# Attention score matmuls: from 128-row operands with zero rows to 32 rows a head, on one Trainium2 core

## The chip, the cores and the metric

The program runs on one core of a Trainium2 chip. Its engines work side by side, each through its own list of instructions in order: TensorE (PE; PEld is its weight load), VectorE (DVE), ScalarE (ACT), GpSimd (POOL) and SyncE (SP), which issues most of the DMAs. They wait for each other through semaphores. The metric is the device time of one execution in microseconds (us); less is better.

## The reference, cut to what matters

One block: gated cross-attention of 16 heads with 8 channels each, over 32 sequences of 128 tokens with 128 channels, and then a gated mixture of experts. The change is in the first part.

```python
B, S, D = 32, 128, 128; H = 16; HD = D // H          # of the inputs used
q = proj(layernorm(x), Wq, bq); k = proj(ctx, Wk, bk); v = proj(ctx, Wv, bv)
scores = jnp.einsum('bhqd,bhkd->bhqk', q, k) / math.sqrt(HD)
scores = jnp.where(m == 0, jnp.float32(-10000000000.0), scores)
p_attn = jax.nn.softmax(scores, axis=-1)
o = jnp.einsum('bhqk,bhkd->bhqd', p_attn, v)         # back to 128 channels
x = x + jnp.tanh(g_xattn[0]) * (o @ Wo + bo)
# then: layernorm, 2 shared and 8 routed experts (two a token), x + tanh(g_ffn[0]) * (...)
```

## The kernel before, in words

**Stages.** A prologue loads x and ctx and finds scales; the attention follows; then the shared experts and the routed experts run with PE nearly always busy. The weights of the experts are loaded and split into two f16 parts during the attention.

**Turns and steps.** The attention works on 16 pairs of sequences. `turns` calls each engine's `body(t, ...)` for turns t = 0 to 19, and each body goes through 8 steps g = 0 to 7 (G = 8). A pair passes through several turns: its q and k are projected at the end of turn t - 1, its plain scores are made from step 2 of turn t + 1 on, its shifted scores from step 7 of turn t + 2 on. A group is 4 heads of one sequence, so a pair has 8 groups and a step handles one plain group and one shifted group. The order on each engine is as the code is written; nothing moves it at run time except the waits.

**What a pair needs.**
- PE transposes x and ctx (L853, L855), ACT copies them out (`XCT`, L645), PE projects q and k (L860, L861, `project_queries_keys`), ACT scales them into `QK32` (L653, `queries_keys`).
- POOL splits them into a high and a low f16 part (L529, L531), then normalises the next pair (L521), adds a bias row (L596), splits weights for the experts (L541, L543, L545, from turn 6 on) and from turn 8 on prepares the rows of the experts (`payload`, L555 to L560), always in this order.
- SP writes the parts to DRAM (`scr`, L453, L455), adds the key mask (L432), and reads them back in another layout: `Q` with 64 rows for two heads (L473) and `K` as two DMAs (L476), each into the half of the rows that belongs to even or odd heads; the other half of `K` stays zero from the start. An f16 row holds high or low parts of one channel, so 32 rows of a head give a product of nearly f32 accuracy. A DMA from Q to Q (L465) clears the rows for the row maxima.
- PE makes the **plain scores** of a group in 4 matmuls (`plain`, L880, into `pS`, two buffers), DVE takes their row maxima (L1257). When the pair's 8 groups are done, PE transposes the maxima (L933), ACT and DVE split them (L676, L1263), and SP puts them into Q as extra rows (L470). The **shifted scores**, transposed (`less`, L880, into `pE`, two buffers), then come out with the row's maximum taken off.
- ACT takes the exponentials (L735, into `PT`, 4 buffers), and PE multiplies them with the values (`values`, L919), two groups every second step, as four 32-column matmuls side by side. The rest of the pair is transposed (L939, L945), projected with Wo (L949) and added to x by DVE (L1276).

**Waits.** A score matmul of group n waits for the maximum or exponential of group n - 2. DVE also computes the inverse deviations for the experts, four linked rounds of small operations in turns 8, 12, 16, 18 and 20 (L1291 to L1302); POOL's payload waits for them.

Of the kernel before, what the change touches and what calls it, by code (L numbers as in the profile page):

```python
# [13 lines left out]
P = 128  # L14
# [20 lines left out]
SLOT_ROWS = 4 * HD  # L35
SHIFT = 2 * SLOT_ROWS
# [10 lines left out]
MASK16 = BIG16 / HD  # L47
# [54 lines left out]
def prologue(nc, io, k):  # L102

    with ExitStack() as ctx:
# [19 lines left out]
        with nc.Block() as block:  # L124
# [11 lines left out]
            def _(g):  # L136
# [6 lines left out]
                g.memset(k.constk[:], BIG16)  # L143
                clear_keys(g, k, 0).then_inc(s.init, 1)
                g.wait_ge(s.init, 1)
                for m in (k.identf, k.ident16):
# [5 lines left out]
                                pattern=[[1, P]], channel_multiplier=-1)  # L152
                for u in range(1, NB - 1):
                    ins = clear_keys(g, k, u)
                ins.then_inc(s.init, 1)
# [17 lines left out]
            def _(v):  # L173
                link = Chain(v, s.dv)
                for u in range(2):
                    link(clear_pair(v, k, u))
                    ins = ones_of_values(v, k, u)
# [21 lines left out]
def clear_keys(g, k, u):  # L199
    return g.memset(k.K[u][:].rearrange("p a b -> p (a b)").bitcast(F32), 0.0)  # L200


def clear_pair(v, k, u):

    v.memset(k.V[u][:].rearrange("p a b c -> p (a b c)"), 0.0)
    return v.memset(k.Q[u][:].rearrange("p a b -> p (a b)").bitcast(F32), 0.0)
# [21 lines left out]
def layer(nc, io, k):  # L228
# [11 lines left out]
    NPT = 4  # L240
# [17 lines left out]
    in_pair = lambda t: t[0:2 * HD].rearrange("p (a b) -> p a b", a=2)  # L258
    MPT = [[in_pair(hi), bg(f"MPl{u}", [2 * HD, 2, S], F16)[:]] for u, hi in enumerate((k.constk, k.constq))]
# [40 lines left out]
    shifts = pA[1][0:2 * HD, 0:2, :]  # L300
# [15 lines left out]
    N_W, N_RD, N_M = 16 * 3, 16 * 4, 16 * 2  # L316
# [11 lines left out]
    head = lambda g, j: 4 * j + g % 4  # L328
# [64 lines left out]
    with nc.Block() as block:  # L393
        @block.sync
        def _(sp):
            head_dim, operand = 4 * W2T, P * 4 * W2T

            def load_tokens(n):
                tiles = slice(CHUNK * n, CHUNK * (n + 1))
                sp.dma_start(k.X[:, tiles, :], io.x.rearrange("b s d -> s b d")[:, tiles, :]).then_inc(k.s_x[n], 16)  # L400
# [27 lines left out]
            def key_mask(t):  # L428
# [3 lines left out]
                sp.dma_start(k.scr[u][1, :, 3, :], k.kmd[t * W2T:(t + 1) * W2T].partition_broadcast(P)).then_inc(s.w[u], 16)  # L432
# [9 lines left out]
            for u in range(NB):  # L442
                if u == NB - 1:
                    sp.wait_ge(s.zk, 1)
                for par in range(2):
                    sp.dma_start(k.K[u][SHIFT + 2 * par:SHIFT + 2 * par + 2, par::2, :], k.constk[:]).then_inc(k.s_padk, 16)

            def body(t, a, b, c, o):
# [10 lines left out]
                if a:  # L459
                    if t == 0:  # L460
                        sp.wait_ge(k.s_pad, 16 * NB)
                    if t == 2:
                        sp.wait_ge(s.z, 1)
                    wait(sp, s.ST, G * (t - NB + 1))
                    sp.dma_start(k.Q[u][SHIFT:SHIFT + 4, :, :], k.Q[u][SHIFT + 4:SHIFT + 8, :, :]).then_inc(s.rd[u], 16)  # L465
                if b:
                    v = (t - 2) % NB
                    for n, done in ((0, s.t2), (1, s.mp)):
                        sp.wait_ge(done, t - 1)
                        sp.dma_start(k.Q[v][SHIFT + n:SHIFT + 4:2, :, :], MPT[t % 2][n].rearrange("p a b -> p (a b)")).then_inc(s.m[v], 16)  # L470
                if a:
                    sp.wait_ge(s.w[u], N_W * again + N_W)
                    sp.dma_start(k.Q[u][0:SHIFT, :, :], scr[0].rearrange("(h2 pd) s t -> (pd s) h2 t", pd=2 * HD)).then_inc(s.rd[u], 16)  # L473
                    for par in range(2):
                        src = scr[1].rearrange("(h2 par d) s t -> par (d s) h2 t", par=2, d=HD)[par]
                        sp.dma_start(k.K[u][SLOT_ROWS * par:SLOT_ROWS * (par + 1), par::2, :], src).then_inc(s.rd[u], 16)  # L476
# [8 lines left out]
                for n in range(2):  # L485
                    if t == TOPS_STORED[n]:
                        store_tops(n)
                for n in {15: range(0, 3), 16: range(3, 6), 17: range(6, NE)}.get(t, ()):
# [27 lines left out]
        def _(g):  # L516
# [59 lines left out]
            def body(t, a, b, c, o):  # L576
                if t < LAG:
                    normalise(t + 1)
                if t == 0:
                    clear_keys(g, k, NB - 1)  # L580
# [1060 lines left out]
```

## Time and profile before

| what | value |
| --- | --- |
| times of 3 runs | 465.22, 465.64, 468.93 us; median 465.64 |
| profiled execution, span from first to last instruction | 464.5 us |
| busy: PE, DVE, ACT, POOL | 392.2, 387.9, 341.6, 316.3 us (84, 84, 74, 68%) |
| DMA | 53.22 MB, mean 115 GB/s |

Only the span of the profiled execution was recorded, not its own device time; the span is 0.7 us under the fastest of the three runs and 1.1 us under their median. Busy shares are means over stages with different limits, so they say little; the stage is read by its own window. In the rows below, "idle" and "waited for" name what ended the wait. Durations of matmuls contain the fill and drain of the array; successive matmuls overlap, so the rate is read from start to start.

### The profile page before, as it was taken

To read this page: it belongs to the slowest core of one execution; us is meant where nothing else is said; L and a number is where in the kernel's file an instruction comes from. 1 tells how busy PE (TensorE), PEld (TensorE's weight loads), DVE (VectorE), ACT (ScalarE), POOL (GpSimd) and SP (SyncE) were. 2 spreads that over 40 slices of the span, in tenths; PEclk is the share of its full clock that TensorE was granted. 3 is DMA by queue.
4 is the path that set the end of the run, shared out by engine and by line. 5 is a ranking of instruction groups with operands and counts; after the bars stand their busy time and mean duration, and the time that the engine had idled before them with its cause. 6 is when DMAs were issued, how large, how long until landed. Compare 5 with 4: busy or idle time off the path is not lost.

```text
span 464.5 us, 13551 instructions
## 1 busy us (share of the span) xinstructions
PE 392.2 (84%) x4611; PEld 297.0 (64%) x4611; DVE 387.9 (84%) x951; ACT 341.6 (74%) x674; POOL 316.3 (68%) x439
## 2 busy tenths in 40 slices
PE   0457998997999899987789897999999999999910
PEld 0335777785887787765534343444699999999910
DVE  7596678978777977799696799777799999999986
ACT  0635687787888788877668657888688888888854
POOL 6242222799899999978777777775067777777750
PEclk9999999999999999999899899999999999999975
DMA  7978884354444253555001111111313333355229
GB/s 190 285 209 222 187 182 107 89 135 95 107 101 105 61 119 92 148 213 185 26 6 53 51 53 46 46 51 55 80 60 93 101 90 97 90 147 171 73 67 295
DMA packets 71825, 53.22 MB, mean 115 GB/s; under 512 B 7481, under 2 KB 63620, under 8 KB 71760
## 3 DMA queue, kind: packets, MB, share of 16 engines
q1 hardware_dynamic: 64752, 43.02, 34.9%
q0 software_dynamic: 4544, 8.44, 5.5%
q10 hardware_dynamic: 2464, 0.91, 0.8%
q8 instruction: 39, 0.64, 0.6%
q14 instruction: 26, 0.21, 0.2%
HBM read 29.38 MB, written 24.33 MB: 116 GB/s over the span
## 4 chain that ended last, share of the span: by engine, by line
PE 46%; DVE 22%; POOL 12%; issue 5%; DMA 5%; ACT 4%; SPq 2%; DVEq 0%; POOLq 0%; ACTq 0%
PE pAtt L1143 11%; PE pAtt L1080 6%; PE pS L1131 5%; PE pE L1131 5%; PE pS L1018 3%; DVE HH L1508 3%; PE pE L1018 3%; DVE t_MX L1257 3%; DMA scr<-QKS 2%; PE pS L880 2%; PE pMix L1121 2%; POOL t_STG L541 2%; POOL t_W2l L545 2%; POOL QKS L531 2%; PE pAtt L919 1%
## 5 line engine op out<-in xcount | busy, mean ns | idle before, releaser
L637 POOL DMA_INDIRECT yd<-Y,XR x78 | 86.8, 1113 | 40.6 <-issue 23.2
L1257 DVE TENSOR_REDUCE t_MX<-pS 128x4 f32<-128x512 f32 x128 | 86.9, 682 | 22.7 <-PE pS L880 20.2
L735 ACT ACTIVATE PT<-pE,t_mbias,t_scl 128x512 f32<-128x512 f32 x128 | 97.0, 789 | 2.9 <-PE pE L880 2.7
L611 POOL DMA_INDIRECT xs<-t_STG,t_pos x64 | 65.6, 1024 | 21.5 <-issue 14.8
L1536 DVE SCALAR_TENSOR_TENSOR HR<-G,t_sc,HR 128x512 f16<-128x512 f32 x78 | 58.6, 751 | 2.8
L1143 PE MATMUL pAtt<-t_W2h,HR 128*128 x624 | 59.2, 219 | 0.8 <-DVE HR L1536 0.7
L880 PE MATMUL pS<-t_K,t_Q 128*128 128x128 f16 x512 | 52.5, 229 | 7.8 <-DVE t_MX L1257 5.1
L1508 DVE SCALAR_TENSOR_TENSOR HH<-H,t_sc,HH 128x512 f16<-128x512 f32 x64 | 48.2, 764 | 8.2 <-ACT HH L789 6.3
L1143 PE MATMUL pAtt<-t_W2l,HR 128*128 x312 | 54.4, 219 | 0.0
L820 ACT ACTIVATE G<-pS,t_b1T,t_inv 128x256 f32<-128x256 f32 x78 | 40.0, 563 | 17.1 <-PE pS L1131 16.1
L880 PE MATMUL pE<-t_Q,t_K 128*128 128x128 f16 x512 | 50.2, 221 | 1.9 <-DMA t_Q<-MPl 1.0
L1143 PEld LDWEIGHTS pAtt<-t_W2h,HR 128*128 128x128 f16 x624 | 49.6, 98 | 1.4 <-issue 1.4
L1080 PE MATMUL pAtt<-HH,t_W2h 128*128 128x512 f16 x128 | 38.4, 381 | 6.8 <-DVE HH L1508 6.8
L880 PEld LDWEIGHTS pS<-t_K,t_Q 128*128 128x128 f16 x512 | 35.6, 103 | 12.6 <-DVE t_MX L1257 7.7
L919 PE MATMUL pAtt<-PT,t_V 128*32 128x128 f32 x1024 | 42.0, 283 | 0.0
L880 PEld LDWEIGHTS pE<-t_Q,t_K 128*128 128x128 f16 x512 | 37.4, 99 | 6.6 <-ACT PT L735 3.4
L820 ACT ACTIVATE G<-pE,t_b1T,t_inv 128x256 f32<-128x256 f32 x78 | 39.9, 569 | 0.0
L1534 DVE TENSOR_SCALAR HR<-G,t_sc 128x512 f16<-128x512 f32 x78 | 37.9, 485 | 0.8 <-ACT G L820 0.2
L529 POOL CAST QKS<-QK 128x512 f16<-128x512 f32 x16 | 9.8, 611 | 42.0 <-ACT QK L653 42.0
L784 ACT ACTIVATE H<-pS,t_b1T,t_inv 128x512 f32<-128x512 f32 x32 | 23.7, 777 | 12.0 <-PE pS L1018 8.0
L1131 PE MATMUL pE<-XE,t_W1h 128*128 128x256 f16 x156 | 32.1, 273 | 0.0
L1131 PE MATMUL pS<-XE,t_W1h 128*128 128x256 f16 x156 | 31.9, 273 | 0.0
(276 smaller groups left out, 1008.6 us busy)
## 6 DMA issues: line engine op xcount, KB each, us to landing
xs<-t_padrow SPq DMA_DIRECT2D x10, 516.0 KB, 5.0
XR<-xs SPq DMA_DIRECT2D x39, 129.0 KB, 2.3
scr<-QKS SPq DMA_DIRECT2D x16, 256.0 KB, 2.4
t_Q<-scr SPq DMA_DIRECT2D x16, 256.0 KB
t_K<-scr SPq DMA_DIRECT2D x32, 128.0 KB
t_STG<-in_W SPq DMA_DIRECT2D x7, 512.0 KB, 6.8
YY<-yd SPq DMA_DIRECT2D x14, 256.0 KB, 4.9
t_X<-in_x SPq DMA_DIRECT2D x4, 512.0 KB, 6.1
```

Of the source, the lines that this page charges most:

```text
L611: g.indirect_dma_start(k.xs, bass.IndirectOffsetOnAxis(ap=pos[:, n:n + 1], axis=0), k.PAY[:, n, :], None).then_inc(h.di[q], 16)
L637: g.indirect_dma_start(k.yd, bass.IndirectOffsetOnAxis(ap=XR[u][:, q, D:ROW], axis=0), Y[u][:, q, :], None, bounds_check=2 * T - 1, oob_is ...
L735: act.activation(PT[:, m % NPT], pE[g % 2][:], ACT.Exp, bias=k.mbias[:, bt:bt + 1], scale=k.scl[:, bt:bt + 1]).then_inc(s.exp, 1)
L820: act.activation(G32[i % 2][:, c, :], pU[c][:, 0:TILE], ACT.Gelu, bias=k.b1T[:, bass.ds(e * NC + c, 1)], scale=k.inv[:, 3:4]).then_inc(r.g ...
L880: ins = pe.matmul(out[:, j, :], ko if transposed else qo, qo if transposed else ko, start=True, stop=True)
L919: ins = pe.matmul(pA[bb][32 * j:32 * j + 32, part // 2, :], k.V[pair % NB][:, 4 * bb + j, part, :], PT[:, m % NPT, j, :], start=(part == 0 ...
L1080: ins = pe.matmul(wide(pA[u]), w[:, w0:w0 + P], HH[e][:, part, c, :], start=(e == 0 and c == 0 and step == 0), stop=(e == 1 and c == NC - ...
L1131: ins = pe.matmul(pU[c][:, 0:TILE], w[:, bass.ds(e * HID + c * P, P)], XE[i % M][:, part, :], start=(step == 0), stop=(step == 2))
L1143: ins = pe.matmul(pA[i % 2][:, q, :], HR[i % M][:, part, c, q * P:(q + 1) * P], w[:, bass.ds(e * HID + c * P, P)], start=(c == 0 and q == ...
L1257: v.tensor_reduce(out=MX[:, n // G % 2, n % G // 4, m % 2, m // 2::2], in_=pS[n % 2][:], axis=AX_X, op=ALU.max).then_inc(s.max, 1)
L1508: v.scalar_tensor_tensor(out=HH[e][:, 1, c, :], in0=H32[:, c, :], scalar=k.sc[:, 2:3], in1=HH[e][:, 0, c, :], op0=ALU.mult, op1=ALU.subtra ...
L1536: v.scalar_tensor_tensor(out=HR[i % M][:, 1, ch, :], in0=G32[i % 2][:, ch, :], scalar=k.sc[:, 2:3], in1=HR[i % M][:, 0, ch, :], op0=ALU.mu ...
```

## The change: what it does

Q and K get one layout: 4 groups of 32 rows, one head in each, 4 heads side by side along the free dimension (`[128, 4, 256]`). A score matmul uses the 32 rows of its head alone, on one of four row groups of the array, and there are no zero rows; the memsets that made them are gone from POOL, DVE and ACT. K comes in one DMA instead of two, and the clearing DMA from Q to Q is gone, since the zeros come with the constants from DRAM: 12 DMAs of 32 KB at the start instead of 4 of 64 KB and 8 small ones. The constants of the mask stand in 4 rows a head instead of 8, so the mask's DMA halves.

`scores(n, m)` replaces `plain` and `less`: it waits for both buffers first and then issues the 4 shifted and 4 plain matmuls in turn, which always lie in different row groups, and signals after the last of each. `values` run four groups at a time at steps 0 and 4 (8 buffers `PT` instead of 4). The projection of q and k, its copy on ACT, the second output projection and the second `residual` move one step later.

```diff
-SLOT_ROWS = 4 * HD
-SHIFT = 2 * SLOT_ROWS
+ROWS = 4
+HEAD_ROWS = P // ROWS
+MASKED = 4
+SHIFT = 4 * HD - 5
...
-    NPT = 4
+    NPT = 8
...
-    N_W, N_RD, N_M = 16 * 3, 16 * 4, 16 * 2
+    N_W, N_RD, N_M = 16 * 3, 16 * 2, 16 * 2
+    SETS = 3
...
+            def fourth(u, op):
+                return k.scr[u][op, :, 3, :].rearrange("(h d) t -> h d t", d=HD)
...
             for u in range(NB):
-                sp.dma_start(k.scr[u][0, :, 3, :], k.constq[:]).then_inc(k.s_pad, 16)
+                sp.dma_start(fourth(u, 0)[:, 0:MASKED, :], k.constq[:]).then_inc(k.s_pad, 16)
+                sp.dma_start(fourth(u, 0)[:, MASKED:HD, :], k.nothing[:]).then_inc(k.s_pad, 16)
+                sp.dma_start(fourth(u, 1)[:, MASKED:HD, :], k.constk[:]).then_inc(k.s_pad, 16)
...
-                    sp.dma_start(k.Q[u][SHIFT:SHIFT + 4, :, :], k.Q[u][SHIFT + 4:SHIFT + 8, :, :]).then_inc(s.rd[u], 16)
...
-                        sp.dma_start(k.Q[v][SHIFT + n:SHIFT + 4:2, :, :], MPT[t % 2][n].rearrange("p a b -> p (a b)")).then_inc(s.m[v], 16)
+                        row = SHIFT + 4 * n
+                        sp.dma_start(k.Q[v][row:row + P - HEAD_ROWS + 1:HEAD_ROWS, :, :], MPT[t % 2][n].rearrange("p a b -> p (a b)")).then_inc(s.m[v], 16)
...
-                    sp.dma_start(k.Q[u][0:SHIFT, :, :], scr[0].rearrange("(h2 pd) s t -> (pd s) h2 t", pd=2 * HD)).then_inc(s.rd[u], 16)
-                    for par in range(2):
-                        src = scr[1].rearrange("(h2 par d) s t -> par (d s) h2 t", par=2, d=HD)[par]
-                        sp.dma_start(k.K[u][SLOT_ROWS * par:SLOT_ROWS * (par + 1), par::2, :], src).then_inc(s.rd[u], 16)
+                    for op, into in ((0, k.Q[u]), (1, k.K[u])):
+                        sp.dma_start(into[:], scr[op].rearrange("(j rd) s t -> (rd s) j t", rd=ROWS * HD)).then_inc(s.rd[u], 16)
...
-                    if g == 6 and 2 <= t < NP - 1:
+                    if g == 7 and 2 <= t < NP - 1:
                         queries_keys(t + 1)
...
+            def score(n, j, out, transposed):
+                g, u = n % G, n // G % NB
+                rows, q = slice(HEAD_ROWS * (g % ROWS), HEAD_ROWS * (g % ROWS + 1)), S * (g // 4)
+                qo, ko = k.Q[u][rows, j, q:q + S], k.K[u][rows, j, q:q + S]
+                return pe.matmul(out[:, j, :], ko if transposed else qo, qo if transposed else ko, start=True, stop=True)
+
+            def scores(n, m):
+                plain, less = 0 <= n < G * NP, 0 <= m < G * NP
+                if less:
+                    if m % G == 0:
+                        pe.wait_ge(s.m[m // G % NB], N_M * (m // G // NB) + N_M)
+                    wait(pe, s.exp, m - 1)
+                if plain:
+                    if n % G == 0:
+                        pe.wait_ge(s.rd[n // G % NB], N_RD * (n // G // NB) + N_RD)
+                    wait(pe, s.max, n - 1)
                 for j in range(4):
...
+                    if less:
+                        to = score(m, j, pE[m % 2], True)
+                    if plain:
+                        of = score(n, j, pS[n % 2], False)
+                if less:
+                    to.then_inc(s.ST, 1)
+                if plain:
+                    of.then_inc(s.S, 1)
...
-                    less(m + 1)
-                    plain(G * (t - 1) + g - PH + 1)
-                    if g % 2 == 0:
-                        values(m - 2)
-                        values(m - 1)
+                    scores(G * (t - 1) + g - PH + 1, m + 1)
+                    if g % 4 == 0:
+                        for n in range(m - 4, m):
+                            values(n)
...
-                    if g == 5 and 2 <= t < NP - 1:
+                    if g == 6 and 2 <= t < NP - 1:
                         project_queries_keys(t + 1)
-                    if g == 5 and o:
+                    if g == 6 and o:
                         project_output(1, t - LAG - 1)
...
-                    if g == 6 and o:
+                    if g == 7 and o:
                         residual(1, pair - 1)
```

How the instructions stand. On **PE**, steps 4 to 6 of an early turn; pE takes shifted and pS plain scores. Before:

```order
L919 MATMUL pAtt<-PT,t_V 32x128 x8
L945 MATMUL pOut<-t_identf,t_AK 128x128
L853 MATMUL pMix<-t_identf,XN 128x128 x2
L855 MATMUL pMix<-t_identf,t_W2l 128x128 x2
L880 MATMUL pE<-t_Q,t_K 128x128 x4
L880 MATMUL pS<-t_K,t_Q 128x128 x4
L860 MATMUL pMix<-XCT,t_Wq 128x256
L861 MATMUL pMix<-XCT,t_Wk 128x256
L949 MATMUL pOut<-t_Wo,t_AT 128x128
```

and with the change:

```order
L907 MATMUL pAtt<-PT,t_V 32x128 x16
L933 MATMUL pOut<-t_identf,t_AK 128x128
L842 MATMUL pMix<-t_identf,XN 128x128 x2
L844 MATMUL pMix<-t_identf,t_W2l 128x128 x2
L870 MATMUL pE<-t_Q,t_K 128x128
L870 MATMUL pS<-t_K,t_Q 128x128
...
L849 MATMUL pMix<-XCT,t_Wq 128x256
L850 MATMUL pMix<-XCT,t_Wk 128x256
L937 MATMUL pOut<-t_Wo,t_AT 128x128
```

The two score rows stand eight times there, that is for steps 5 and 6: a whole step of scores now lies between the transposes and the projections, which lay behind the scores of step 5.

On **SP**, the DMAs of one early turn. Before:

```order
L453 DMA scr<-QKS 128x2x512
L455 DMA scr<-QKS 128x2x256
L432 DMA scr<-kmd 128x256
L465 DMA t_Q<-t_Q 4x2048
L470 DMA t_Q<-t_constk 2x8x256
L470 DMA t_Q<-MPl 2x8x256
L473 DMA t_Q<-scr 64x8x256
L476 DMA t_K<-scr 32x8x256 x2
```

and with the change:

```order
L447 DMA scr<-QKS 128x2x512
L449 DMA scr<-QKS 128x2x256
L429 DMA scr<-kmd 16x4x256
L462 DMA t_Q<-t_constk 4x4x256
L462 DMA t_Q<-MPl 4x4x256
L466 DMA t_Q<-scr 128x4x256
L466 DMA t_K<-scr 128x4x256
```

Two of nine DMAs a turn are gone, and the mask's is half as large.

## Rows read from the trace of the kernel before

**Rows 1.** Busy us by engine in six stretches; the first line names the columns.

```profile
core 0: us, PE busy (x) PEld busy (x) DVE busy (x) ACT busy (x) POOL busy (x), PEclk, DMA share, GB/s
52.30:83.10 30.80, 27.95 (x421) 22.62 (x418) 24.64 (x60) 24.30 (x51) 9.69 (x15) 1.00 0.73 168
83.10:115.80 32.70, 28.64 (x439) 23.23 (x428) 28.57 (x76) 24.93 (x52) 30.32 (x55) 1.00 0.43 102
115.80:201.20 85.40, 81.25 (x1277) 66.63 (x1275) 67.65 (x180) 71.78 (x153) 77.09 (x137) 1.00 0.44 110
201.20:226.30 25.10, 20.02 (x331) 15.20 (x331) 23.34 (x84) 18.88 (x38) 19.14 (x38) 0.93 0.41 151
219.50:222.90 3.40, 0.98 (x11) 0.90 (x11) 3.08 (x13) 0.70 (x3) 2.76 (x7) 1.00 0.07 19
222.90:226.40 3.50, 3.32 (x46) 2.22 (x44) 3.13 (x15) 3.11 (x7) 1.68 (x5) 0.51 0.00 0
```

**Rows 2.** POOL's waits, 84 to 202 us: total us, times, longest.

```profile
POOL t_XF L555 <- DVE t_nmr L1302: 1.8, 2, 1.5
...
POOL QKS L529 <- ACT QK L653: 0.3, 1, 0.3
```

**Rows 3.** POOL in order of time, one turn: start, us, line and instruction.

```profile
128.29 0.89 POOL L555 TENSOR_SCALAR t_XF<-t_X,t_rstd,t_nmr 128x128 f32<-128x128 f32 x2 [0.18 <-POOL t_W2l L545]
...
130.32 0.61 POOL L529 CAST QKS<-QK 128x512 f16<-128x512 f32 x1
...
139.27 0.88 POOL L555 TENSOR_SCALAR t_XF<-t_X,t_rstd,t_nmr 128x128 f32<-128x128 f32 x2 [0.18 <-POOL t_W2l L545]
```

**Rows 4.** ACT in order of time, the copy that L529 waits for.

```profile
127.63 1.04 ACT L653 ACTIVATE QK<-pMix,t_bqk,t_sc 128x256 f32<-128x256 f32 x2
```

**Rows 5.** The chain that ended last, 52 to 84 us: start, us, what.

```profile
54.27 3.95 DMA scr<-QKS
...
59.58 0.45 SPq L476
...
61.27 2.81 SPq L416
...
64.61 5.46 DMA scr<-QKS
...
71.44 4.63 DMA t_K<-scr
...
81.64 0.68 DVE t_MX L1257
```

**Rows 6.** SP in order of time, 53 to 73 us: the clearing DMA.

```profile
65.72 0.67 SPq L465 DMA_DIRECT2D t_Q<-t_Q  x1
```

**Rows 7.** PE in order of time, step 0 of one turn.

```profile
129.39 0.40 PE L880 MATMUL pE<-t_Q,t_K 128*128 128x128 f16 x4
129.63 0.39 PE L880 MATMUL pS<-t_K,t_Q 128*128 128x128 f16 x4
129.94 0.65 PE L919 MATMUL pAtt<-PT,t_V 128*32 128x128 f32 x16
130.52 0.40 PE L958 MATMUL pMix<-t_ident,t_STG 128*128 128x128 f16 x4
```

**Rows 8.** PE's waits, 83.2 to 202 us, for the load of K.

```profile
PE pS L880 <- DMA t_K<-scr: 1.0, 1, 1.0
```

**Rows 9.** The chain that ended last, 14 to 39 us.

```profile
15.28 4.61 DVE t_mx L196 x4
...
37.20 0.85 PE pMix L861 x2
38.05 0.44 PE pS L880 x4
```

**Rows 10.** SP in order of time, 20 to 29 us: constants at the start.

```profile
20.48 2.39 SPq L439 DMA_DIRECT2D scr<-t_constq  x4
...
23.58 5.40 SPq L446 DMA_DIRECT2D t_K<-t_constk  x8
```

More of the change, by code:

```diff
@@ L46 @@
 BIG16 = 32768.0
-MASK16 = BIG16 / HD
+MASK16 = BIG16 / MASKED
 class Parts(dict):
@@ L151, in _ @@
                 g.affine_select(out=k.lower[:], in_=k.lower[:], compare_op=ALU.is_gt, fill=0.0, base=0,
[L152 to L155, printed above, removed]
+                                pattern=[[1, P]], channel_multiplier=-1).then_inc(s.init, 1)
                 g.wait_ge(s.init, 2)
@@ L874, in _ @@
             pe.matmul(bias_cols, bvr[:], k.Wo[:], start=True, stop=True).then_inc(s.any, 1)
-            def scores(g, u, out, transposed):
-                for j in range(4):
-                    hd, q = head(g, j), S * (g // 4)
-                    qo, ko = k.Q[u][:, hd // 2, q:q + S], k.K[u][:, hd, q:q + S]
-                    ins = pe.matmul(out[:, j, :], ko if transposed else qo, qo if transposed else ko, start=True, stop=True)
-                return ins
-            def plain(n):
-                if not 0 <= n < G * NP:
-                    return
-                pair, g = n // G, n % G
-                if n == 0:
-                    pe.wait_ge(k.s_padk, 32 * NB)
-                if g == 0:
-                    pe.wait_ge(s.rd[pair % NB], N_RD * (pair // NB) + N_RD)
-                wait(pe, s.max, n - 1)
-                scores(g, pair % NB, pS[n % 2], False).then_inc(s.S, 1)
@@ L895, in less @@
-            def less(m):
-                if not 0 <= m < G * NP:
-                    return
-                pair, g = m // G, m % G
-                if g == 0:
-                    pe.wait_ge(s.m[pair % NB], N_M * (pair // NB) + N_M)
-                wait(pe, s.exp, m - 1)
-                scores(g, pair % NB, pE[m % 2], True).then_inc(s.ST, 1)
+            def score(n, j, out, transposed):
[3 more added lines that the diff above has]
+                return pe.matmul(out[:, j, :], ko if transposed else qo, qo if transposed else ko, start=True, stop=True)
@@ L1599, in program @@
         k.s_c, k.s_x = ([outer.enter_context(nc.semaphore(f"{n}{c}")) for c in range(NT // CHUNK)] for n in ("c_ctx", "c_x"))
-        k.s_one, k.s_pad, k.s_padk, k.s_b2, k.s_rest = (outer.enter_context(nc.semaphore("c_" + n)) for n in ("one", "pad", "padk", "b2", "rest"))
+        k.s_one, k.s_pad, k.s_b2, k.s_rest = (outer.enter_context(nc.semaphore("c_" + n)) for n in ("one", "pad", "b2", "rest"))
         k.keep = outer
-        alloc(outer, k, MX=([P, 2, 2, 2, HD], F32), PV=([P, 2, 2, S], F32),
+        alloc(outer, k, MX=([P, 2, 2, ROWS, 4], F32), PV=([P, 2, 2, S], F32),
               REC=([P, 2, H], F32), AK=([P, 2, H, HD], F32), AT=([P, 2, S], F32), ST6=([P, 2, 6], F32), XF=([P, 2, D], F32),
```

44 lines of the change are left out of this document (16 added, 28 removed).

## The prediction, made before the changed kernel was run

> **What bounds the kernel now.** I cut the attention into stretches and read the busy times in each first [rows 1]. PE looks like the bound of all of them: 27.95 of 30.8 us, 28.64 of 32.7, 81.25 of 85.4. But POOL is as full between 83.1 and 201.2 us: 30.32 of 32.7 and 77.09 of 85.4. To tell which of two full engines leads, I read who waits for whom. From 84 to 202 us POOL waits 1.8 us for DVE's inverse deviations and 0.3 us for the copy of q and k, and for nothing else but itself [rows 2]. An engine that stands still for 2 us in 118 runs at its own pace. Its order of time shows that pace: the same instruction stands at 128.29 and at 139.27 us, a turn of 10.98 us [rows 3]. Its little gaps are linked operations waiting for each other, and the change does not touch POOL's list there. PE's work is 81.25 / (85.4 / 10.98) = 10.45 us a turn, 0.5 us less than POOL's: PE follows.
>
> Before 83.1 us POOL has little to do (9.69 of 30.8 us), so something else leads there. The chain that ended last runs from 54 to 76 us through SP and DMAs: the write of the parts 3.95 us, issues of K, of weights and of the maxima (2.81 us), the next write 5.46 us, the load of K 4.63 us [rows 5]. PE, 91% busy in that stretch, appears in it only at the end. After 201.2 us DVE leads: 23.34 of 25.1 us [rows 1]. So the change speeds up the engine that is fullest, and that leads in none of the three stretches.
>
> **The change part by part.**
>
> *Scores on 32 rows.* A group's four matmuls start 129.63 - 129.39 = 0.24 us before the next four, so a step's eight take 0.48 us and a turn's 64 take 3.84 us [rows 7]; their weight loads are already hidden, since that is 0.06 us each. The trace has no matmul on a row group, so the price is bounded: if the two row groups do not overlap, nothing is saved; if they overlap fully, half, 1.92 us a turn. The nearest row is the values: 16 matmuls on four column groups start and are over in 0.58 us, four side by side [rows 7]. I take nearly the full 1.9 us. The Trainium skill, "TensorE: Matmul & The Clock Gate", Part 3, says the same of row groups: matmuls on different ones run at once, four tiles measured 3.07 times faster. No run here shows it yet.
>
> *Values four groups at a time.* A block of two takes 0.58 us, and 0.07 us are lost before it (0.31 from the plain scores to the values against 0.24 between two sets of scores) [rows 7]. Half as many blocks save four such losses, 0.3 us a turn. A block of four makes PE deaf to scores for 1.2 us; ACT and DVE have up to two finished groups in their buffers, about 1.4 us of work.
>
> *Changes between tile shapes.* Before, only the values differ in shape: four blocks, eight changes a turn. Now scores (32 rows), values (32 columns) and all other matmuls (full) differ from each other: counted in the new order, three changes at steps 0 and 4, two at 1, 2, 3 and 6, 14 a turn. At 0.07 us, six more cost 0.4 us; at a whole matmul's 0.24 us [rows 7], 14 x 0.24 - 8 x 0.07 = 2.8 us. I take 0.4 us, the row of a change of shape. In sum PE has 1.9 + 0.3 - 0.7 (the four value losses are in both counts, so I keep a margin) = 1.5 us a turn less to do, about 9 us a turn.
>
> *What this is worth from 83.1 to 201.2 us:* nothing by itself, POOL's 10.98 us stand. At most the 1.8 us that POOL waits for DVE can go, because DVE gets its maxima sooner: 0 to 1.8, I take 1.3 us. DVE has the room, 28.57 of 32.7 us.
>
> *Projections one step later.* A step is 10.98 / 8 = 1.4 us. POOL needs the copy of q and k at 130.32 us and has it at 127.63 + 1.04 = 128.67 us [rows 3, 4]: 1.65 us to spare, more than a step, and PE gains on it. Cost there nothing. Late next, if that cover were gone, is POOL's L529, with the split weights behind it: the excess over 1.65 us would be paid in each of some nine turns.
>
> *SP.* K's second issue is gone: 0.45 us in the chain in turn 3, and again before the load of K in turn 4, 0.9 us in all [rows 5]. The clearing DMA's 0.67 us issue [rows 6] lies beside the 5.46 us write that SP waits for anyway: nothing. The bytes of a turn are nearly the same. Against the 0.9 us stands the later projection in turn 5: now behind the scores of step 6, which wait for the maximum that DVE ends at 81.64 + 0.68 us [rows 5]. That may cost up to a step, 1.4 us, less what the faster scores give back. For the stretch before 83.1 us: from a loss of 1.4 us to a gain of 3 turns x 1.9 = 5.7 us if PE led after all. I take a gain of 0.3 us, near the SP rows, since the chain names SP.
>
> *Prologue.* The memsets of K, Q and constants lie beside the loads of ctx; the chain from 15 to 38 us is DVE's maxima, PE and ACT [rows 9]. Nothing. The constants' DMAs: 4 took 2.39 us and 8 took 5.40 us to issue, 7.8 us; 12 at 0.60 to 0.68 us take 7.2 to 8.1 [rows 10]. They end before the first scores, which stand directly behind the projection of pair 2 on PE [rows 9]. Nothing.
>
> *The last pair.* Once in 118 us PE waited for the load of K, 1.0 us [rows 8]; with one issue less I take 0.5 us (0 to 1.0).
>
> *The end, 201.2 to 226.3 us:* DVE's idle time is 25.1 - 23.34 = 1.76 us, the most that faster scores can give. I take 0.7 us. What follows starts that much earlier and is not changed.
>
> **Sum.** 0.3 + 1.3 + 0.5 + 0.7 = 2.8 us. The span was 464.5 us, 1.1 us under the median of the runs, 465.64; taken off that, 462.8 us. By the bounds: 465.64 + 1.4 = 467.0 at one end, 465.64 - 5.7 - 1.8 - 1.0 - 1.8 = 455.3 at the other.
>
> **The rivals.**
>
> *PE led before 83.1 us.* For it: 91% busy, more than any other engine there. Against: the chain. Then 3 x 1.5 to 1.9 us come off early and all of POOL's work moves forward; with 1.8 + 0.5 to 1.0 + 0.7 to 1.8 us behind: 7.5 to 10.3 us less, 455.3 to 458, say 456.8. Chance 0.20.
>
> *No overlap of row groups.* Then PE saves only 0.3 us a turn, and shape changes take that back. POOL still leads; what stays is SP's part, 0.5 to 1 us: 465. For it: no row shows a row group at work. Chance 0.17.
>
> *Slower: shape changes make PE the leader.* For it: 14 changes against 8, and scores stand between nearly all other matmuls. It decides from the point where PE's turn passes 10.98 us, 0.5 us more than now. At 0.24 us a change and no overlap, PE's turn is 10.45 + 2.8 = 13.2 us, 2.3 us over POOL's in 7.8 turns, and as much in the three early ones: some 20 us; at half that price and no overlap, 10.45 + 1.1 = 11.6 us, 0.6 us in some ten turns, 6 us. So 472 to 485, say 474. Against: the 0.07 us row. The Trainium skill, "TensorEngine Tiling (Array Packing)", section "Tiling Modes", has this rule: a change of tiling mode, not just of the tile, drains TensorE. The values' 0.07 us shows a loss of that kind, though a small one. Chance 0.11.
>
> *The clock falls.* PE was 0.98 of 3.4 us busy from 219.5 us, and the next 3.4 us had a granted clock of 0.51 of 2.4 GHz, that is 1.2 GHz [rows 1]. If a PE with less to do fell so once a turn, 3.4 us at half speed take 1.7 us of its work; PE's 9 us become 10.7, still under 10.98. So it matters only if it stays low, and then PE's turn is near 18 us and the time over 550. Against: at 9 us a turn PE would still be over 80% busy, and a stretch at 28.64 of 32.7 us held 1.00. Chance 0.03.
>
> **The numbers.** The forecast, POOL leads and PE's gain turns into waiting: 0.49, with its own range 459.5 to 465. The likeliest time is 462.8 us. About 1%, 4.7 us, is what a measurement here can tell from no change, so faster begins at 461.0. Of the forecast a quarter lies there (0.13), with the 0.20 of the first rival: 0.33. Slower is the third rival and the fourth, 0.14. The rest, 0.53, is the same. A range from 456.0 to 468.5 leaves out the slow cases and part of the early gain, together 0.2.
>
> **What the profile would show.** Right, if POOL's turn stays at 10.98 us with no new wait for L653, PE's busy share between 83 and 201 us falls from 95% toward 85%, and PE's new idle time is put down to POOL's L521 or to the load of K. Scores: eight starts within 0.25 to 0.3 us, pE and pS nearly together; if they still take 0.48 us, the rows do not overlap. Shape changes: the start-to-start time from scores to the next full matmul and back; over 0.2 us speaks for the slower rival. DVE's wait at L555 should go from 1.8 us toward 0. I am wrong if POOL's list starts its turn 6 over 2 us before 83.1 us, if POOL waits for L653 in the middle turns, or if the granted clock drops below 1.00 before 219 us.

## The result and the profile after

The changed kernel took 475.91 us (median of 4 runs, 471.89 to 478.14); the kernel before 465.88 us beside it. The ratio is 1.022, with a 95% interval of 1.015 to 1.029: 2.2% slower, outside the range that was given (456.0 to 468.5 us). Four further runs, taken later, gave 476.44 us, 1.027 (1.020 to 1.034). Medians here are of all runs; ratios and their intervals leave out runs more than 1.5% above the fastest of the same kernel. Engines and clock of the profiled execution (span 476.3 us, 478.14 us by its own time), from the page; each digit is a fortieth of the span:

```profile
PE 396.5 (83%) x4611; PEld 285.0 (60%) x4611; DVE 383.0 (80%) x949; ACT 339.8 (71%) x672; POOL 307.9 (65%) x436
...
PEclk9999999896899689855589999999999999999975
```

The granted clock of the kernel before, for comparison:

```profile
PEclk9999999999999999999899899999999999999975
```

PE's busy time rose by 4 us although its scores take half as long. The second line goes with that: the granted clock has dips that the kernel before does not have. The same in stretches of the clock's record, busy us by engine:

```profile
core 0: us, PE busy (x) PEld busy (x) DVE busy (x) ACT busy (x) POOL busy (x), PEclk, DMA share, GB/s
...
83.90:87.30 3.40, 3.40 (x52) 2.39 (x50) 3.37 (x10) 1.80 (x3) 2.23 (x4) 0.50 0.00 0
107.80:111.20 3.40, 2.52 (x33) 1.39 (x32) 3.19 (x10) 2.87 (x9) 3.33 (x6) 1.00 0.41 126
111.20:121.50 10.30, 8.09 (x82) 5.99 (x83) 7.99 (x26) 4.96 (x10) 7.83 (x16) 0.50 0.20 58
121.50:159.00 37.50, 31.91 (x574) 23.33 (x568) 28.02 (x73) 32.89 (x72) 34.62 (x62) 1.00 0.31 90
155.60:159.00 3.40, 2.26 (x36) 1.33 (x32) 3.19 (x10) 3.06 (x10) 3.25 (x7) 1.00 0.39 120
159.00:169.30 10.30, 9.00 (x93) 6.67 (x97) 7.08 (x21) 5.36 (x10) 6.78 (x13) 0.50 0.19 56
...
200.00:240.90 40.90, 39.85 (x449) 28.03 (x440) 28.93 (x104) 25.66 (x51) 27.96 (x52) 0.50 0.38 134
```

Four stretches, 65 us together, stand at 0.50, that is 1.2 GHz. Ahead of the second and third PE had little to do: 2.52 and 2.26 of 3.4 us, while DVE had 3.19 in both, in turns 8 and 12 with their rounds of inverse deviations. But little work alone does not bring a fall. Here are a stretch of the kernel before, in turn 8 too, and another of the changed kernel; the clock fell behind neither:

```profile
107.80:111.20 3.40, 2.36 (x39) 1.88 (x38) 3.19 (x10) 2.60 (x7) 3.19 (x7) 1.00 0.95 207
```

```profile
128.20:131.60 3.40, 2.37 (x28) 1.82 (x26) 1.50 (x4) 3.23 (x7) 3.02 (x7) 1.00 0.54 158
```

In the last of the four PE is busy for 39.85 of 40.9 us: at half speed it leads the tail, in which DVE led before [rows 1].

The clock was also late. Its record begins at 52.3 us before and at 60.0 us after; the windows print 1.00 ahead of that, which is no measurement. Matmuls in order of time tell it:

```profile
55.32 0.31 PE L870 MATMUL pE<-t_Q,t_K 32*128 32x128 f16 x1
55.35 0.31 PE L870 MATMUL pS<-t_K,t_Q 32*128 32x128 f16 x1
55.42 0.31 PE L870 MATMUL pE<-t_Q,t_K 32*128 32x128 f16 x1
...
134.10 0.27 PE L933 MATMUL pOut<-t_identf,t_AK 128*128 128x128 f32 x1
134.30 0.23 PE L870 MATMUL pE<-t_Q,t_K 32*128 32x128 f16 x1
134.31 0.22 PE L870 MATMUL pS<-t_K,t_Q 32*128 32x128 f16 x1
134.37 0.21 PE L870 MATMUL pE<-t_Q,t_K 32*128 32x128 f16 x1
...
134.48 0.21 PE L870 MATMUL pS<-t_K,t_Q 32*128 32x128 f16 x1
134.63 0.44 PE L927 MATMUL pAtt<-t_identf,t_PV 128*128 128x128 f32 x2
```

At 55 us two pE scores start 0.10 us apart, at 134 us 0.06 to 0.07: half clock, then full. The rows show two more things. pE and pS start together, so the row groups overlap: eight scores take 0.24 us, not 0.48. And a change of shape has a price: the first score starts 0.20 us after a transpose, the next transpose 0.15 us after the last score. In the kernel before, where both have 128 rows, it was 0.11:

```profile
131.25 0.27 PE L945 MATMUL pOut<-t_identf,t_AK 128*128 128x128 f32 x1
131.36 0.39 PE L880 MATMUL pE<-t_Q,t_K 128*128 128x128 f16 x4
```

That is 0.09 us for the way there, where 0.07 was taken; the way back costs as much, 0.15 against the 0.06 between two scores.

POOL's casts of q and k after, as in [rows 3]:

```profile
132.55 0.61 POOL L521 CAST QKS<-QK 128x512 f16<-128x512 f32 x1
...
143.49 0.60 POOL L521 CAST QKS<-QK 128x512 f16<-128x512 f32 x1
...
154.42 0.61 POOL L521 CAST QKS<-QK 128x512 f16<-128x512 f32 x1
168.31 0.61 POOL L521 CAST QKS<-QK 128x512 f16<-128x512 f32 x1 [2.76 <-ACT QK L644]
```

At full clock POOL's turn is 10.94 us, with no wait. The turn that holds the fall at 159 us takes 13.9 us (11.1 before), and POOL waits 2.76 us for the copy.

To find where the time went, I took the same marks from the traces: the start of POOL's cast of a pair, the end of the last exponential, the end of the span. They begin at pair 2, since executions differ by 1 to 1.5 us ahead of it. The runs named keep, keep from 5 and steps back are experiments below.

| us between marks | before | after | after, again | keep | keep from 5 | keep, steps back, less tail |
| --- | --- | --- | --- | --- | --- | --- |
| cast of pair 2 to 6 | 43.9 | 45.9 | 45.9 | 46.0 | 46.3 | 45.4 |
| 6 to 12 | 69.5 | 69.4 | 69.0 | 69.1 | 69.9 | 73.4 |
| 12 to 13 | 11.1 | 13.9 | 12.6 | 12.3 | 12.2 | 12.5 |
| 13 to 15 | 22.0 | 22.5 | 21.9 | 21.9 | 21.9 | 21.9 |
| 15 to last exponential | 39.7 | 47.4 | 46.5 | 43.0 | 40.0 | 41.5 |
| to the end | 239.2 | 238.1 | 238.0 | 237.5 | 239.4 | 239.2 |
| low clock from 60 to 241 us | 3.4 | 64.9 | 47.8 | 3.4 | 0 | 13.7 |

The spans differ by 11.7 us (476.25 against 464.53). Of these 7.7 are lost in the tail, 2.8 in the turn of pair 12, 2.0 in the first turns and 0.5 behind pair 13; 1.1 come back at the end.

The tail can be followed through four executions without any added matmuls in it. With 13.7 us of low clock between the cast of pair 15 and the last exponential it took 41.9 us (warm start, an experiment below), with 23.9 us 44.2 (apart, below), with 34.7 us 46.5 (after, again) and with 38.1 us 47.4 (after). In the kernel before it was 39.7 us with 2.4.

### The profile page after: what moved, and what is told of

Its sections match the earlier page's. It is cut to its first block, busy times and chain, and to the rows that moved or that the text cites. A ratio compares the mean times of both kernels' runs of the same rounds, so it can differ in the third digit from the quotient of the medians.

```text
span 476.3 us, 13605 instructions
## 1 busy us (share of the span) xinstructions
PE 396.5 (83%) x4611; PEld 285.0 (60%) x4611; DVE 383.0 (80%) x949; ACT 339.8 (71%) x672; POOL 307.9 (65%) x436
## 4 chain that ended last, share of the span: by engine, by line
PE 61%; DVE 16%; ACT 8%; issue 7%; DMA 2%; POOL 1%; SPq 0%; ACTq 0%; POOLq 0%; DVEq 0%
PE pAtt L1130 9%; PE pAtt L907 8%; PE pE L870 6%; PE pAtt L1067 5%; PE pS L1118 5%; PE pE L1118 5%; ACT PT L724 4%; DVE HH L1495 3%; PE pS L1006 3%; PE pE L1006 3%; PE pMix L849 3%; DVE t_MX L1244 3%; PE pMix L850 2%; PE pMix L1108 2%; PE pOut L937 1%
## 5 line engine op out<-in xcount | busy, mean ns | idle before, releaser
L870 PE MATMUL pE<-t_Q,t_K 32*128 32x128 f16 x512 | 55.4, 242 | 22.7 <-ACT PT L724 17.4
L870 PEld LDWEIGHTS pE<-t_Q,t_K 32*128 32x128 f16 x512 | 33.6, 103 | 45.9 <-ACT PT L724 29.9
L1495 DVE SCALAR_TENSOR_TENSOR HH<-H,t_sc,HH 128x512 f16<-128x512 f32 x64 | 48.2, 764 | 7.8 <-ACT HH L778 5.9
L870 PE MATMUL pS<-t_K,t_Q 32*128 32x128 f16 x512 | 51.3, 243 | 1.9 <-DVE t_MX L1244 1.9
L907 PE MATMUL pAtt<-PT,t_V 128*32 128x128 f32 x1024 | 43.7, 324 | 0.0
L809 ACT ACTIVATE G<-pE,t_b1T,t_inv 128x256 f32<-128x256 f32 x78 | 39.7, 567 | 0.0
L907 PEld LDWEIGHTS pAtt<-PT,t_V 128*32 128x32 f32 x1024 | 32.1, 129 | 5.1 <-issue 2.0
L870 PEld LDWEIGHTS pS<-t_K,t_Q 32*128 32x128 f16 x512 | 30.2, 102 | 5.1 <-DVE t_MX L1244 3.8
```

The costliest lines, as they stand in the source:

```text
L809: act.activation(G32[i % 2][:, c, :], pU[c][:, 0:TILE], ACT.Gelu, bias=k.b1T[:, bass.ds(e * NC + c, 1)], scale=k.inv[:, 3:4]).then_inc(r.g ...
L870: return pe.matmul(out[:, j, :], ko if transposed else qo, qo if transposed else ko, start=True, stop=True)
L907: ins = pe.matmul(pA[bb][32 * j:32 * j + 32, part // 2, :], k.V[pair % NB][:, 4 * bb + j, part, :], PT[:, m % NPT, j, :], start=(part == 0 ...
L1495: v.scalar_tensor_tensor(out=HH[e][:, 1, c, :], in0=H32[:, c, :], scalar=k.sc[:, 2:3], in1=HH[e][:, 0, c, :], op0=ALU.mult, op1=ALU.subtra ...
```

## The experiments

**First four: undo one part each, or give PE its time back.** Theories: C, the granted clock; W, new waits (one wait for both scores, blocks of four); P, the later projection.

*Twice*: every score matmul issued twice.

```diff
-                for j in range(4):
+                for j in (0, 1, 2, 3) * 2:
                     if less:
                         to = score(m, j, pE[m % 2], True)
```

> The changed kernel, but every score matmul is issued a second time into the same place: PE gets the time back that the row groups saved (eight starts 0.24 us, sixteen 0.48 us) and nothing else moves. Theory C (the granted clock: a PE with less to do falls to 1.2 GHz in places, for 64 us between 84 and 241 us in the profile after, and is warm only from 60 instead of 52 us): the low stretches before 241 us shrink to under 25 us in all and the time is 460 to 467 us. Theory W (the new waits: scores wait for both buffers, values block PE for four groups): more work in the same waits, 476 us or more. Theory P (the later projection makes POOL wait 13.2 us for the copy of q and k): unchanged waits, 474 to 480 us.

488.02 us, 1.047 (1.037 to 1.056). The time is in theory W's range and against theory C as it was put: the low clock between 84 and 241 us did shrink, to 13.6 us, and the time rose. PE had its full clock at 63.9 us only, and then led: POOL's cast waits for the copy in every turn, which takes 11.67 us:

```profile
140.77 0.61 POOL L521 CAST QKS<-QK 128x512 f16<-128x512 f32 x1 [0.68 <-ACT QK L644]
152.44 0.61 POOL L521 CAST QKS<-QK 128x512 f16<-128x512 f32 x1 [0.67 <-ACT QK L644]
```

*Steps back*: the four calls at their old steps.

```diff
-                    if g == 6 and 2 <= t < NP - 1:
+                    if g == 5 and 2 <= t < NP - 1:
                         project_queries_keys(t + 1)
...
```

> The changed kernel with the projection of q and k, its copy, the second output projection and the second residual at their old steps. Theory P: POOL's 13.2 us of waits for the copy of q and k fall below 4 us, 464 to 467 us. Theory C: PE has as little to do as before, the clock falls as often, 470 to 478 us. Theory W: nothing of the waits for ACT and DVE goes, 473 to 478 us.

471.38 us, 1.014 (1.007 to 1.020); of its five runs four took 469.4 to 472.8 us and one 482.45. Between the theories. The four had a mean clock of 0.950 to 0.965, those of the changed kernel 0.914 to 0.942, so this does not separate P from C. Keep, steps back, below, does so for turn 12.

*Blocks of two*: values as before, two groups every second step.

```diff
-                    if g % 4 == 0:
-                        for n in range(m - 4, m):
+                    if g % 2 == 0:
+                        for n in range(m - 2, m):
                             values(n)
```

> The changed kernel with the values two groups at a time at every second step. Theory W: steps are even again, ACT's exponentials and DVE's maxima do not stop while a block of 1.0 us runs, 464 to 468 us. Theory C: PE's work is the same within 0.3 us a turn, low clock for as long as in the changed kernel (over 50 us before 241 us), 470 to 478 us. Theory P: 474 to 478 us.

481.13 us, 1.034 (1.027 to 1.040): slower than the changed kernel and outside all three ranges. The blocks of four are no loss.

*Apart*: shifted scores first, then plain ones, each behind its own wait.

```diff
-                    scores(G * (t - 1) + g - PH + 1, m + 1)
+                    scores(-1, m + 1)
+                    scores(G * (t - 1) + g - PH + 1, -1)
```

> The changed kernel with the shifted scores of a step issued first, behind their own wait, and the plain scores then behind theirs, as in the kernel before; rows and layout as changed. If the row groups overlap only between neighbours of different groups, eight starts take 0.45 us again instead of 0.24, PE is busier, and theory C expects less low clock than in the changed kernel and 464 to 471 us; if they overlap anyway, theory C expects 470 to 478 us. Theory W (one wait for both): 464 to 468 us whatever the clock does. Theory P: 474 to 478 us.

477.03 us, 1.028 (1.021 to 1.035): theory W falls, as far as one wait for both scores goes. The trace shows why the order within a step is free. Issued four and four, pE and pS still start side by side:

```profile
133.07 0.22 PE L870 MATMUL pE<-t_Q,t_K 32*128 32x128 f16 x1
133.09 0.23 PE L870 MATMUL pS<-t_K,t_Q 32*128 32x128 f16 x1
133.14 0.21 PE L870 MATMUL pE<-t_Q,t_K 32*128 32x128 f16 x1
133.15 0.21 PE L870 MATMUL pS<-t_K,t_Q 32*128 32x128 f16 x1
```

**The next four: the layout alone, and matmuls on all rows.** *Rows only* joins the last three edits, so that only the layout is left. *Rows only, twice* adds the doubling. *Whole first* puts matmuls on all 128 rows into the changed kernel, in steps with plain scores alone too, *rows only, whole* into the layout alone. Theory O says that the moves together cost, theory R that matmuls on 32 rows leave the clock low:

```diff
+                for j in range(4):
+                    if less:
+                        whole(m, j, pE[m % 2], True)    # score() with all 128 rows
                 for j in range(4):
                     if less:
                         to = score(m, j, pE[m % 2], True)
```

> The changed kernel with the whole order of the kernel before: projections at their old steps, values two groups at a time, shifted scores ahead of plain ones with waits of their own. Only the layout with 32 rows a head (and its DMAs and buffers) is left of the change. Theory O (the three moves together cost, each alone is covered by the others): 462 to 468 us. Theory C (PE has less to do, the granted clock falls and PE stays at 1.2 GHz longer at the start): low clock as long as in the changed kernel, first full clock after 58 us, 469 to 478 us.

> The one before with every score matmul issued twice, so that PE spends as long on scores as in the kernel before, on 32 rows. Theory O: PE's turn is as before, 464 to 469 us. Theory C as it stood (the clock follows how long PE works): clock as in the kernel before, 464 to 469 us. Theory R (it is matmuls on 32 rows that leave the clock low, as the doubling showed, where PE worked without a break and got the full clock only at 63.9 us): first full clock after 58 us, 472 to 488 us.

> The changed kernel with four matmuls on all 128 rows ahead of the eight of each step, into the place that the shifted scores then overwrite: PE's time for scores is that of the kernel before (0.24 + 0.24 us a step), as with the doubling, but half of it on all rows. Theory R: full clock from 52 to 56 us on, under 20 us of low clock between 84 and 241 us, 462 to 472 us. Theory O, and a theory that only PE's time counts: as the doubling, 480 to 492 us.

> The layout alone, in the order of the kernel before, with the four matmuls on all rows ahead of the shifted scores of each step. Theory R: clock as in the kernel before, 462 to 467 us, and clearly under the one without them. Theory O: PE has 0.24 us more a step than without, 464 to 470 us, no better than without them.

Rows only: 483.9 us, 1.042 (1.033 to 1.051), so the moves as a whole are worth 8 us under the new layout; theory O (the moves cost) falls, and theory C's 478 us is passed too. Its clock came at 79.7 us and was low for 41 us up to 243 us.

Rows only, twice: 562.0 to 600.8 us in four runs (median 589.6), far beyond any expectation. The profiled execution took 579.0 us. Its busy times by engine, and below them PE in order of time:

```profile
64.00:260.00 196.00, 196.00 (x1907) 147.38 (x1905) 83.12 (x205) 83.40 (x164) 76.92 (x137) 1.00 0.19 55
```

```profile
140.77 0.31 PE L870 MATMUL pE<-t_Q,t_K 32*128 32x128 f16 x1
140.86 0.31 PE L870 MATMUL pS<-t_K,t_Q 32*128 32x128 f16 x1
140.88 0.31 PE L870 MATMUL pE<-t_Q,t_K 32*128 32x128 f16 x1
```

PE was busy for all of 196 us and stayed at 1.2 GHz: pE starts 0.11 us apart, and the clock's record begins at 260.0 us. The printed 1.00 of that stretch, and with it this run's mean of 0.985, is a default. The Trainium skill, "TensorE: Matmul & The Clock Gate", Part 1, says that the slow clock is the default state and that activity releases it. This trace shows that being busy is not enough: with scores on 32 rows a full PE stayed slow, and in the kernel before, on 128 rows, it was fast from 52.3 us. But rows are not the whole of it. *Twice*, with the same doubled scores in the changed kernel's order, was at full clock from 63.9 us; what in the order makes this difference was not tested.

Rows only, whole: 477.8 us, 1.029 (1.022 to 1.036), 6 us faster than rows only although 32 matmuls a turn were added. Theory R's clock holds, and that the added matmuls win time, but not its 462 to 467 us. Nearly all of the 6 us lies behind the last exponential (237.6 us against 243.2, where rows only had its clock low until 243.5 and for 6.9 us more later): in the attention the held clock and the added work nearly cancel. From 67.0 to 459.5 us its clock never fell:

```profile
PEclk9999999999999999999999999999999999999985
```

At full clock it shows the price of the shapes: PE leads, a turn of POOL takes 11.64 us (casts at 149.52 and 161.16 us, the second behind a wait of 0.65 us for the copy), against 10.98 before with the same score time. It has 20 changes of shape a turn against 8; 12 more at 0.09 us are 1.1 us on PE's 10.45. Whole first: 490.1 us, 1.055 (1.047 to 1.063), in the range of the theory that only PE's time counts and not in R's, although the full clock came at 57.9 us and fell three times for 3.4 us only before 241 us: work added in every step makes PE lead. So it must be added only where PE waits.

**Four that hold the clock in places.** *Keep*: eight whole matmuls a step in turns 8, 12 and 16 to 18, between the two waits. *Warm start*: 128-row matmuls where PE waits from 16 to 52 us. *Both*, and the warm start in the kernel before. Theory C is now that the granted clock sets the loss, theory W2 that the uneven steps of the new order do. `fill` stands in several places, with 6 to 20 matmuls:

```diff
+    KEEP = {8: 8, 12: 8, 16: 8, 17: 8, 18: 8}
...
                     wait(pe, s.exp, m - 1)
+                    for j in range(KEEP.get(m // G + LAG, 0)):
+                        whole(m, j % 4, pE[m % 2], True)
                 if plain:
...
+                    fill(8)    # warm start: ident16 by ident16 into pE[0], ahead of early waits
```

> The changed kernel with eight extra matmuls on all 128 rows a step in turns 8, 12, 16, 17 and 18 (the turns in which the clock fell), between the wait for the exponential and the wait for the maximum, into the place that the shifted scores overwrite. Nothing else is changed. Theory C (the granted clock sets the loss): the early stretch stays as in the changed kernel (full clock from about 60 us), low clock between 100 and 241 us goes from 61 us to under 15, and with it the 2.7 us lost at 159 to 169 and the 7.7 us at 200 to 241: 462 to 468 us. Theory W2 (the uneven steps of the new order set PE's turn, the clock only follows): 474 us or more, since PE gets work added.

> The changed kernel with extra 128-row matmuls where PE waits between 16 and 52 us, so that it is busy on all rows before the scores begin. Theory C: full clock before 35 us, projections of the first pairs in half the time, POOL's split of pair 6 by 79 to 83 us instead of 84.9; the later falls stay: 468 to 474 us. Theory W2: the early chain through SP and DMAs and the uneven steps set the pace, pair 6 within 1 us of 84.9, 474 to 479 us.

> The changed kernel with the extra matmuls of both, and four a step in turns 3 and 4. Theory C: full clock from before 35 us to the end but for under 20 us, 456 to 464 us, faster than the kernel before. Theory W2: 472 us or more.

> The kernel before with the same extra matmuls between 16 and 52 us. Theory C: full clock before 35 us instead of 52.3, the prologue's projections in half the time, 458 to 463 us. Rival (the prologue's chain hides PE): 464 to 467 us, the same.

Keep: 470.62 us, 1.010 (1.004 to 1.016): more work on PE, and half of the loss is gone. Three of its four runs took 469.3 to 470.7 us; in the fourth, 479.26 us, the mean clock was 0.951 instead of 0.978 to 0.979. In the profiled execution, after 85.6 us the clock did not fall before 450 us. Theory W2's 474 us or more falls; the time is 2.6 us over theory C's upper end, and the table says where: the first turns, pair 12, and a tail of 43.0 us.

Warm start: 477.85 us, 1.026 (1.018 to 1.033). The full clock came at 27.7 us and fell at 38.0 us, as the first scores began, until 48.2; pair 6 came 3.8 us later than before. Both: 481.02 us, 1.032 (1.028 to 1.037); low from 37.2 to 71.3 us. These two miss theory C's numbers, and their times are those of W2: the clock could not be kept through the first scores in this way. The kernel before with the warm start: 469.12 us, 1.007 (1.004 to 1.010). Its clock fell at 37.1 us too, with scores on 128 rows, but only until 40.5. Pair 2's copy ended 5.0 us sooner there, yet the first exponential moved from 51.81 to 50.66 us only, about what its execution was ahead at the first copy (1.2 us). The rival was right that an earlier clock wins nothing ahead of 52 us, though the time is over its 464 to 467 us.

**Six for what was left.** *Again* is the changed kernel unaltered. *Keep, steps back* joins keep with the old steps. *Keep, steps back, less tail* has four instead of eight in turns 16 to 18. *Early four* adds fill(4) to it in the steps with plain scores alone. *Keep from 5*, without the old steps, has `KEEP = {5: 4, 6: 4, 8: 8, 12: 8, 16: 4, 17: 4, 18: 4}`, and *keep 12* has `{12: 8}`.

> The changed kernel once more, unaltered, on one chip with the three that follow, so that they can be compared with it. Every theory: 472 to 478 us, low clock for over 30 us between 84 and 241 us and full clock first at about 58 to 60 us.

> The extra matmuls in turns 8, 12 and 16 to 18, as before, and the projections, the copy and the second residual at their old steps. Theory P as what is left beyond the clock (POOL still waited 1.7 us in three waits for the copy of q and k in turns 8 to 13): 466 to 468 us. If the later step costs nothing: 469 to 472 us, as with the extra matmuls alone.

> As the last, with four instead of eight extra matmuls a step in turns 16 to 18. If the extra work itself costs in the tail (PE was busy for 34.56 of 36 us from 196 us on): 1 to 3 us less than the last, 464 to 467 us. If four do not hold the clock in the tail: low clock for over 10 us after 196 us and 468 us or more.

> As the last, with four extra matmuls on all rows in each step that has plain scores alone (38 to 49 us), while PE waits for DVE's maximum. If the clock rises there as in the kernel before: full clock before 54 us, pair 6 split 1 to 2 us earlier, 462 to 466 us. If it does not: 0.4 us a step added, 466 us or more.

> The changed kernel with all its moves and extra matmuls on all rows: four a step in turns 5, 6 and 16 to 18, eight in 8 and 12. Theory C: no low clock between 70 and 240 us (also not the 3.4 us at 82, the 13.7 us at 86 that cost 4.3 us in two other runs), 464 to 468 us; no faster than the kernel before, since POOL's turn of 10.98 us leads from 84 us on and the 2 us of the first turns at half clock stay. If the extra matmuls in turns 5 and 6 cost more than the clock gives: 470 us or more.

> The changed kernel with the eight extra matmuls in turn 12 alone. Theory C: no low clock from 153 to 175 us, POOL's split of pair 13 loses 1.3 us or less against pair 12 (2.7 in the changed kernel), the falls before and in the tail stay, 471 to 476 us. If the fall in turn 12 does not matter: 2.5 us lost there all the same.

Again: 476.44 us, as expected. Over its runs and the first four, time follows the clock: low clock, worked out as (1 - mean clock) x span / 0.5, was 55 to 56 us in the three runs of 471.9 to 474.0 us and 80 to 92 us in the four of 477.9 to 479.6 (the eighth run: 64 us, 473.7); in the kernel before it is 23 us.

Keep, steps back: 477.09 us, 1.024 (1.016 to 1.031), worse than keep; less tail: 473.52 us, 1.019 (1.012 to 1.025); both miss their ranges. Theory P falls here for turn 12: POOL's wait for the copy went, and a wait of 1.7 us for DVE's deviations came in its place (0.2 us in keep). But these two show a fall that costs much. The one with less tail is at half clock from 86.0 to 99.6 us, keep from 5 is not; they also differ in the steps, and in four added matmuls a step in turns 5 and 6. POOL's casts and the busy times of the stretch, first with the fall:

```profile
83.20 0.61 POOL L522 CAST QKS<-QK 128x512 f16<-128x512 f32 x1 [7.06 <-ACT QK L645]
...
99.10 0.61 POOL L522 CAST QKS<-QK 128x512 f16<-128x512 f32 x1 [4.69 <-ACT QK L645]
```

```profile
86.00:99.60 13.60, 13.45 (x124) 8.79 (x117) 8.97 (x19) 8.25 (x17) 8.26 (x18) 0.50 0.37 111
```

and without it:

```profile
83.91 0.61 POOL L522 CAST QKS<-QK 128x512 f16<-128x512 f32 x1 [8.42 <-ACT QK L645]
...
95.48 0.61 POOL L522 CAST QKS<-QK 128x512 f16<-128x512 f32 x1 [0.32 <-ACT QK L645]
```

```profile
86.00:99.60 13.60, 12.63 (x215) 9.37 (x214) 11.56 (x28) 11.41 (x25) 12.49 (x26) 1.00 0.45 139
```

15.90 us against 11.57: with a fall of 13.6 us the turn took 4.3 us more; PE was busy for 13.45 of 13.60 us and POOL stood still for 4.69 us. A fall does not always cost that. The changed kernel itself had 12.6 us of low clock between pairs 6 and 12 and took 69.4 us there, keep 69.1 with 2.0.

Early four: 480.48 us, 1.026 (1.018 to 1.035): the clock came at 55.6 us and fell again at 59.0; a miss. Keep 12: 474.83 us, 1.019 (1.015 to 1.023), as theory C expected; pair 12's turn took 12.7 us at full clock instead of 13.9, so the fall of 10.3 us in it was worth 1.2 us. In the second profile of the changed kernel ("after, again") the fall there was of 3.4 us, and the turn took 12.6.

Keep from 5: 471.54 us, 1.016 (1.009 to 1.023), its profiled execution 469.26 us. It is over the 464 to 468 us expected, no better than keep, and no version here beats the kernel before. But its trace has no low clock from 58.7 to 241 us, and the tail is back at 40.0 us. Its busy times there:

```profile
196.00:232.00 36.00, 32.93 (x575) 24.71 (x572) 31.06 (x110) 26.77 (x54) 28.65 (x53) 1.00 0.44 158
```

The chain of the tail, one block of values, first in the changed kernel and then in keep from 5:

```profile
219.35 1.86 PE pAtt L907 x32
```

```profile
213.11 1.01 PE pAtt L917 x32
```

## Why the prediction was wrong, point by point

Two of its three signs of being wrong came: POOL waited for the copy of q and k in the middle turns, and the clock was low long before 219 us. The third, POOL's turn 6 starting early, did not: the cast of pair 6 came at 84.99 us.

- **PE's saving: right.** Eight scores take 0.24 us instead of 0.48. The rival without overlap is out.
- **Shape changes: right in kind, a little small.** 0.09 us instead of 0.07; 14 against 8 changes cost some 0.5 us a turn, not 0.4. The rival that they alone make PE lead is out: at full clock POOL's turn stayed at 10.94 us. That its 474 us lie near the measured time is a coincidence. The Trainium skill, "TensorEngine Tiling (Array Packing)", section "Tiling Modes", says that a change of tiling mode drains TensorE; the trace shows a loss of that kind, 0.09 us at the changes read above.
- **POOL leads from 84 us: right up to pair 12.** From pair 6 to 12 the changed kernel took 69.4 us, before 69.5, although 12.6 us of it were at half clock. PE's gain bought nothing there.
- **Projections one step later: right in sum.** POOL's waits for the copy grew, as these rows of its waits from 84 to 202 us say; 8.0 us of them end at pair 6, where it waited 8.1 us before as well:

```profile
POOL QKS L521 <- ACT QK L644: 13.2, 5, 8.0
...
POOL t_XF L547 <- DVE t_nmr L1289: 0.5, 2, 0.2
```

  The wait for DVE shrank as forecast [rows 2], but the 1.3 us were not gained: the wait for the copy, longest under half clock, stood in its place.
- **The clock rival: the step that failed.** It had a chance of 0.03. Its price of a short fall held: the execution in the column "after, again" had two falls of 3.4 us between pairs 6 and 12 and took 69.0 us there. Three things in it were wrong. It took PE's busy share as what holds the clock, with a stretch at 28.64 of 32.7 us as evidence [rows 1]; the doubled scores show a PE that is always busy and slow. Between falls of 3.4 us once a turn, covered by POOL's turn, and a clock that stays low for good it saw nothing; falls of 10.3 us and one of 40.9 came, in the turns with DVE's rounds and in the tail, where PE waits for DVE. And it did not ask who leads at half speed in the tail: 20.02 us of PE's work in a tail of 25.1 us [rows 1] is near 40 us then, and PE was busy for 39.85. Held at full clock, the tail takes 40.0 us instead of 47.4 and pair 12's turn 12.2 to 12.7 instead of 13.9. Why the clock falls with this kernel and not with the one before is shown only in part: not for lack of work alone, and matmuls on all rows hold it.
- **First turns: 2.0 us lost instead of 0.3 won.** The full clock came 7.7 us later, and the chain ran through PE at half speed (a block of values 1.87 us at 56.93 us, 1.06 at 63.43). The loss sits between the casts of pairs 3 and 4, from 52.60 to 63.78 us: 11.2 us against 8.8 before. Every variant with 32-row scores lost 1.4 us or more in the first turns, whatever its steps. That the late clock is all of it was not shown, since no experiment brought the clock forward without other cost.
- **The tail: 0.7 us won was forecast, 7.7 were lost.** With the clock held it takes 0.3 and 1.8 us more than in the kernel before with four added matmuls a step, 3.3 with eight.

Open: the 1.1 us that pair 12's turn keeps at full clock, and whether added matmuls on 32 rows, in those turns alone, would hold the clock in turns 8, 12 and 16 to 18 as well. That wasn't tried; *twice*, which adds them in every step, cut the low clock between 84 and 241 us from 65 to 13.6 us.

## What to carry to other kernels

When a change takes work or rows from TensorE, do not stop at "it does not lead": look for each stretch in which it waits for others, ask whether its clock stays up there, and work out who leads if it halves. Read the clock stretch by stretch, and ahead of its first record by the spacing of matmuls, not by a mean. Time freed on an engine that does not lead is worth nothing, and here it was worth less than nothing.

## What was not expected of the hardware

- A TensorE that was busy without a break for 196 us, with its scores on 32 rows and doubled, stayed at 1.2 GHz; with four 128-row matmuls a step instead of the doubling, the clock was full from 67.0 us and never fell until 459.5. The same doubling in another order of the instructions was at full clock from 63.9 us.
- Row groups overlap even when the program issues four matmuls of one and then four of another: the second four start 0.01 to 0.02 us after the first four, one by one.
- Going from 128-row to 32-row matmuls or back cost 0.09 us at full clock, at the places read here.
